# Ranking tokens for a top-64 selection: scores spread by TensorE, comparisons by key, counts as products with ones

## The reference

```python
def _L2_xattn_ref(query_seq, value_seq, router_w, q_w, kv_w, out_w):
    ...
    rw = jnp.einsum('bsd,od->bs', query_seq, router_w).astype(jnp.float32)
    top_w, top_idx = jax.lax.top_k(rw, C)
    resampled = jnp.take_along_axis(query_seq, top_idx[:, :, None], axis=1)
    q = jnp.einsum('bcd,ed->bce', resampled, q_w)
    ...
    q = q * _rope_factor(q_pos, d)
    ...
    att = jnp.einsum('bce,de->bcd', att, out_w)
    src = att * top_w[:, :, None]
    out = jnp.zeros_like(query_seq).at[jnp.arange(B)[:, None], top_idx].set(src)
    return out
```

## Time and profile before

| what | value |
|---|---|
| time, median of 3 runs | 2991.71 us |
| the three runs | 2980.21, 2994.35 and 2991.71 us |
| time of the profiled execution | 2995.15 us |
| span of the profiled execution | 2993.4 us |
| mean granted TensorE clock over the span | 0.893 of full speed |

### The profile page before, as it was taken

The page is one execution under the profiler, slowest core; times in us unless marked ns, Lnnn a source line. Parts: engine busy times, 40 slices in busy tenths (PEclk is TensorE's granted clock), DMA queues, the critical chain, the costliest instruction groups (busy, mean ns, idle before and its releaser), DMA issues. The chain is left out here.

```text
span 2993.4 us, 46160 instructions
## 1 busy us (share of the span) xinstructions
PE 2414.1 (81%) x16128; PEld 1491.5 (50%) x16128; DVE 1610.1 (54%) x3751; ACT 1283.7 (43%) x2885; POOL 922.6 (31%) x907
## 2 busy tenths in 40 slices
PE   2973676767667997899759889879999998399698
PEld 1432455345533444566437656546666665245465
DVE  5766764466455774333465444445555554566433
ACT  1652565346523665222224322246666665135222
POOL 2312772277203330000000000036777777054000
PEclk7986898789977998899879789989999999589799
DMA  5610000000004330000010000010000000042000
GB/s 140 79 18 6 1 1 1 0 1 1 1 8 103 44 43 1 15 0 0 0 48 1 1 30 0 0 62 1 1 1 1 1 1 1 11 46 33 1 0 14
DMA packets 49811, 53.80 MB, mean 18 GB/s; under 512 B 9264, under 2 KB 47920, under 8 KB 48720
## 3 DMA queue, kind: packets, MB, share of 16 engines
q1 hardware_dynamic: 42992, 41.68, 8.3%
q0 software_dynamic: 4896, 8.81, 1.0%
q10 hardware_dynamic: 1728, 0.79, 0.2%
HBM read 24.25 MB, written 1.05 MB: 8 GB/s over the span
## 5 line engine op out<-in xcount | busy, mean ns | idle before, releaser
L1958 POOL TENSOR_SCALAR L3x_prob<-L3x_prob,L3x_inverse 128x512 f32<-128x512 f32 x256 | 396.4, 1566 | 182.8 <-DVE L3x_inverse L2136 182.8
L1076 DVE TENSOR_TENSOR W_probT<-W_prob,W_pS 128x512 f32<-128x512 f32 (+1 forms) x232 | 159.4, 687 | 367.4 <-ACT W_prob L1059 367.4
L1059 ACT ACTIVATE W_prob<-W_pS 128x512 f32<-128x512 f32 (+1 forms) x232 | 138.6, 597 | 457.7 <-PE W_pS L1030 457.7
L1040 PEld LDWEIGHTS W_pT<-fw,W_probT 128*128 128x128 f32 (+1 forms) x1856 | 242.0, 191 | 116.0 <-issue 107.5
L1029 PE MATMUL W_pS<-hT,fw 128*128 (+1 forms) x464 | 242.8, 605 | 26.1 <-DVEq L497 26.1
L1040 PE MATMUL W_pT<-fw,W_probT 128*128 128x128 f32 (+1 forms) x1856 | 246.2, 276 | 6.2 <-DVE W_probT L1076 6.2
L2098 DVE CUSTOM_DVE_ANT_0 L3x_prob<-L3x_pS,L3x_mask_now 128x512 f32<-128x512 f32 x256 | 166.1, 686 | 149.0 <-PE L3x_pS L1966 149.0
L1030 PE MATMUL W_pS<-hT,fw 128*128 (+1 forms) x464 | 240.0, 599 | 0.0
L2043 ACT ACTIVATE L3x_prob<-L3x_prob,L3x_row_top 128x512 f32<-128x512 f32 x256 | 183.2, 717 | 72.3 <-DVE L3x_row_top L2098 72.3
L871 DVE TENSOR_REDUCE L1x_row_top<-L1x_pS 128x2 f32<-128x1024 f32 x128 | 156.6, 1223 | 73.5 <-PE L1x_pS L686 72.9
L815 ACT ACTIVATE L1x_prob_by_key<-L1x_pX 128x512 f32<-128x512 f32 x256 | 148.6, 597 | 100.9 <-PE L1x_pX L693 99.8
(11 more groups left out here) (370 smaller groups left out, 5183.0 us busy)
## 6 DMA issues: line engine op xcount, KB each, us to landing
L0x_key_stack<-xw SPq DMA_DIRECT2D x48, 128.0 KB
L1x_key_stack<-xw SPq DMA_DIRECT2D x96, 64.0 KB
L3f_stacks<-L3f_qk_part SPq DMA_DIRECT2D x96, 64.0 KB
fw<-in_f_L3f SPq DMA_DIRECT2D x1, 4483.5 KB, 13.5
fw<-in_f_L1f POOLq DMA_DIRECT2D x1, 4359.0 KB, 18.9
fw<-in_f_L0f POOLq DMA_DIRECT2D x1, 3890.0 KB, 15.4
fw<-in_f_L2f SPq DMA_DIRECT2D x1, 3460.0 KB, 10.8
L0x_query_stack<-xw SPq DMA_DIRECT2D x42, 64.0 KB
```

Source lines behind the costliest of these rows:

```text
L1040: last = pe.matmul(m.pT[:, e % 2, t * C:(t + 1) * C], hidden[0:size, s, t * P:(t + 1) * P], down(i), start=i == 0 and t == 0, stop=i == PI ...
L1059: act.activation(gated[0:size, s, 0:GROUP], prod[0:size, s, :], func, bias=bias).then_inc(activated, 1)
L1076: ins = dve.tensor_tensor(hidden[0:size, s, 0:GROUP], gated[0:size, s, 0:GROUP], prod[0:size, 2 + s, :], ALU.mult)
L1958: pool.tensor_scalar(prob(u, h, t), prob(u, h, t), m.inverse[:, u % 2, h, t:t + 1], None, ALU.mult).then_inc(a.normed, 1)
```

## The change

The router's row becomes a 128 x 128 table whose columns are all the same, so that one set of four products with `hT` gives every token's score in every partition at once. DVE still picks the own scores out with the identity. Comparisons now have the other direction: partition `p` holds a key, and its 0/1 row says which tokens it precedes. They are made of `across` (keys of one tile against tokens of the other), `within` (the same tile, strict) and `ties` (same tile, equal, and an earlier key, by a 128 x 128 table `sooner` in place of `earlier`). They are written as 2-byte numbers, and TensorE sums them over the keys by products with a column of ones, 48 products into 16 columns of the bank `pG`. A copy of these columns is the rank. `sel`, its transposes, the projection and the rotary product go by groups of four tiles.

```diff
     "L1x": [("wq", C), ("wk", C), ("wv", C), ("wo", C), ("bq", 1), ("bk", 1), ("bv_row", C), ("bo_row", C)],
-    "L2x": [("wq", C), ("wk", C), ("wv", C), ("wo", C), ("router_row", C), ("l2_ropeq", QT * C),
-            ("l2_ropek", SK), ("own_head", L2_HEADS // 2), ("slot", 2 * L2_CAP), ("earlier", QT * S)],
+    "L2x": [("wq", C), ("wk", C), ("wv", C), ("wo", C), ("router_wide", C), ("l2_ropeq", QT * C),
+            ("l2_ropek", SK), ("own_head", L2_HEADS // 2), ("slot", 2 * L2_CAP), ("sooner", P)],
...
+        every = m.banks.rearrange("p a n -> p (a n)").rearrange("p (b t j) -> p b t j", b=B, t=QT)
+        own = m.route[:, :].rearrange("p (b t) -> p b t", t=QT)
+        part = lambda n: m.kT[:, 2 * n:2 * n + 2, :].rearrange("p c n -> p (c n)").bitcast(BF16)[:, 0:TOK].rearrange(
+            "p (b t j) -> p b t j", b=B, t=QT)
+        across, within, ties = part(0), part(1), part(2)
+        same = m.v[:, 0, 0:TOK // 2].rearrange("p (b t j) -> p b t j", b=B // 2, t=QT)
...
         def _(pe):
-            pe.wait_ge(diagonal, 1)
             for g in range(4):
-                last = pe.matmul(m.banks[:, g, :], m.ones[:, :], wide(m.h)[:, g * 512:(g + 1) * 512], start=True,
-                                 stop=True)
+                last = pe.matmul(m.banks[:, g, :], w["router_wide"], m.hT[:, g * 512:(g + 1) * 512], start=True, stop=True)
             last.then_inc(spread, 1)
-            pe.wait_ge(picked, 1)
+            pe.wait_ge(compared, 1)
+            for b in range(B):
+                for t in range(QT):
+                    at = b * QT + t
+                    pe.matmul(m.pG[:, at:at + 1], across[:, b, t, :], m.onesb[:, 0:1], start=at == 0, stop=False,
+                              skip_group_check=True)
+                    pe.matmul(m.pG[:, at:at + 1], within[:, b, t, :], m.onesb[:, 0:1], start=False, stop=False,
+                              skip_group_check=True)
+            for half in range(2):
+                pe.wait_ge(tied, half + 1)
+                for b in range(4 * half, 4 * half + 4):
+                    for t in range(QT):
+                        at = b * QT + t
+                        last = pe.matmul(m.pG[:, at:at + 1], ties[:, b, t, :], m.onesb[:, 0:1], start=False, stop=True,
+                                         skip_group_check=True)
+            last.then_inc(ranked, 1)
             for g in range(4):
+                pe.wait_ge(picked, g + 1)
                 for t in range(4):
                     last = pe.transpose(m.banks[:, g, t * P:(t + 1) * P], sel[:, 4 * g + t, :], m.k["ident"])
                 last.then_inc(turned, 1)
...
-            last.then_inc(queries, 1)
+                last.then_inc(queries, 1)
...
-            st.done(dve.tensor_tensor(m.h[:, :, :], m.xn[:, :, :], row(w["router_row"], TILES), ALU.mult))
-            st.done(dve.tensor_reduce(m.route[:, :], m.h[:, :, :], AX_X, ALU.add))
-            dve.tensor_tensor(m.h[:, :, :], ident, each(m.route[:, :], P), ALU.mult).then_inc(diagonal, 1)
             dve.wait_ge(spread, 1)
-
-            st.done(dve.tensor_tensor(m.o[:, :, :], m.banks.rearrange("p a (t c) -> p (a t) c", c=P), ident,
-                                      ALU.mult))
-            st.done(dve.tensor_reduce(m.own[:, :], m.o[:, :, :], AX_X, ALU.add))
-            own = each(m.own[:, :].rearrange("p (b t) -> p b t", t=QT), S)
-            for b in range(2):
-                at = slice(4 * b, 4 * b + 4)
-                other = every[:, at, :].unsqueeze(2).broadcast_to([P, 4, QT, S])
-                mine = own[:, at]
-                for n in range(4):
-                    st.done(dve.tensor_tensor(more[:, 4 * b + n], other[:, n], mine[:, n], ALU.is_gt))
-                    st.done(dve.tensor_tensor(same[:, 4 * b + n], other[:, n], mine[:, n], ALU.is_equal))
-            earlier = w["earlier"].rearrange("p (t j) -> p t j", t=QT).unsqueeze(1).broadcast_to([P, B, QT, S])
-            st.done(dve.tensor_tensor(same, same, earlier, ALU.mult))
-            st.done(dve.tensor_tensor(more, more, same, ALU.add))
-            st.done(dve.tensor_reduce(m.own[:, :].rearrange("p (b t) -> p b t", t=QT), more, AX_X, ALU.add))
-            dve.tensor_tensor(sel, row(w["slot"], TILES), each(m.own[:, :], 2 * L2_CAP), ALU.is_equal).then_inc(picked, 1)
+            st.done(dve.tensor_tensor(m.o[:, :, :], m.banks.rearrange("p a (t c) -> p (a t) c", c=P), ident, ALU.mult))
+            st.done(dve.tensor_reduce(m.route[:, :], m.o[:, :, :], AX_X, ALU.add))
+            dve.tensor_tensor(across[:, :, 0, :], every[:, :, 0, :], each(own[:, :, 1], P), ALU.is_lt)
+            dve.tensor_tensor(across[:, :, 1, :], every[:, :, 1, :], each(own[:, :, 0], P), ALU.is_le)
+            dve.tensor_tensor(within, every, each(own, P), ALU.is_lt).then_inc(compared, 1)
+            sooner = w["sooner"].unsqueeze(1).unsqueeze(1).broadcast_to([P, B // 2, QT, P])
+            for half in range(2):
+                at = slice(4 * half, 4 * half + 4)
+                st.done(dve.tensor_tensor(same, every[:, at], each(own[:, at], P), ALU.is_equal))
+                last = dve.tensor_tensor(ties[:, at], same, sooner, ALU.mult)
+                last.then_inc(tied, 1)
+                dve.wait_ge(tied, half + 1)
+            dve.wait_ge(ranked, 1)
+            st.done(dve.tensor_copy(m.own[:, :], m.pG[:, 0:TILES]))
+            for g in range(4):
+                at = slice(4 * g, 4 * g + 4)
+                dve.tensor_tensor(sel[:, at, :], row(w["slot"], 4), each(m.own[:, at], 2 * L2_CAP),
+                                  ALU.is_equal).then_inc(picked, 1)
             turn_out_dve(dve, m, selT, turned, copied)
-            dve.wait_ge(queries, 1)
-            rope = w["l2_ropeq"].rearrange("p (n) -> p n").unsqueeze(1).broadcast_to([P, B, QT * C])
-            dve.tensor_tensor(wide(m.h).rearrange("p (b n) -> p b n", b=B),
-                              m.banks.rearrange("p a (b n) -> p (a b) n", b=2), rope, ALU.mult)
+            for g in range(4):
+                dve.wait_ge(queries, g + 1)
+                rope = w["l2_ropeq"].rearrange("p (n) -> p n").unsqueeze(1).broadcast_to([P, 2, QT * C])
+                dve.tensor_tensor(wide(m.h).rearrange("p (b n) -> p b n", b=B)[:, 2 * g:2 * g + 2, :],
+                                  m.banks[:, g, :].rearrange("p (b n) -> p b n", b=2), rope, ALU.mult).then_inc(roped, 1)
...
-                     tile2(k_at < q_at)]
+                     part[:, None] < part[None]]
...
-        "x_L2x": [L2x["q_w"].T, L2x["kv_w"][:C].T, L2x["kv_w"][C:].T, L2x["out_w"].T, rows(L2x["router_w"]),
+        "x_L2x": [L2x["q_w"].T, L2x["kv_w"][:C].T, L2x["kv_w"][C:].T, L2x["out_w"].T, rows(L2x["router_w"]).T,
```

More of the change, by code:

```diff
@@ L1632, in select_phase @@
     with Phase(nc, "L2x_select") as ph:
[L1633 to L1637, removed]
+        steps, spread, compared, tied, ranked, picked, turned, copied, queries, roped = (ph.sem(n) for n in (
+            "steps", "spread", "compared", "tied", "ranked", "picked", "turned", "copied", "queries", "roped"))
```

## The result

| | before | after |
|---|---|---|
| runs side by side on one chip | 4 | 4 |
| median | 2987.6 us (2980.21 to 2994.35) | 2952.45 us (2946.7 to 2962.18) |
| ratio, with its 95% interval | | 0.9892 (0.9863 to 0.992) |
| profiled execution | 2995.15 us | 2953.88 us |
| its span, mean granted clock | 2993.4 us, 0.893 | 2951.3 us, 0.906 |

The kernel is 35 us faster between the medians, and the interval of the ratio leaves out 1.

The account below looks back on a forecast made before the run. The selection was taken as one chain of DVE and TensorE in turn, 32.45 us in place of 55.16; with 1.0 behind it, 23.7 us less, 2971.4 profiled, 2968 as a median. Range 2956 to 2979 us.

Parts of the forecast that it names:

- the base: Whole kernel before: profiled 2995.15 us, 3.4 above the median of 2991.71, from which the gain was taken.
- Link 5: Selection, last eight ties: TensorE's products not hidden under DVE, with a semaphore, 1.1 us.
- Link 8: Selection, projection and rotary product: products 4.95 us, the mean of four examples, 5.7 with the last rotary quarter.
- Link 3: Selection, comparisons across and within: three DVE instructions from PSUM, 4.85 us.
- links 1, 2, 4, 6 and 7: Selection: spread 5.6 us, own scores 4.65, ties 5.05, copy of the ranks 0.3, slots and transposes 5.2.
- Link 9: Start of the attention behind the selection: shorter TensorE idle time, possibly a higher clock, gains 1.0 us.
- signs of being wrong: Wrong if comparisons exceed 1.3 ns a column, counts 0.126 us apart, or any later phase changes over a few us.
- Counts don't overlap: Selection: products adding into one column run one after another, costing 8.95 us more: 2977 us, chance 0.08.
- Clock stays low: Projection at the low clock's 6.97 us costs 2.0 more, next phase gains nothing: 2971 us, chance 0.12.
- Clock high throughout: Spread, last ties, transposes, products and next phase at the upper clock, 7 us less: 2961 us, chance 0.06.
- Gain swallowed: Selection: comparisons and ties, 9.9 us, cost 3.3 times that, bringing the time back to 2991 us; chance 0.05.
- Slower: Attention of the chosen tokens: clock held at 0.50, costing up to 120 us: 3088 us, chance 0.02.

Follow-up runs that it names:

- after, once more: The changed kernel, unedited, run again in more rounds against the kernel before: 2952.81 us, ratio 0.9901.
- counts only: The changed kernel with the old spread and without the groups of four, so only comparison by key and counts are new: 2975.09 us, ratio 0.9963.
- groups only: The kernel before with only slots, transposes, projection and rotary product by groups of four tiles: 2974.58 us, ratio 0.9956.
- more counts: The changed kernel with 320 more products with ones, into columns nobody reads: 2961.43 us, ratio 0.992.
- own scores by bank: The changed kernel with own scores picked out as each bank fills: 2951.43 us; with one DVE addition behind the last rotary quarter as well: 2950.27 us.
- old tables: The changed kernel with 384 columns of zeros behind its tables, giving them their old size: 2952.47 us, ratio 0.9902.
- null before: The kernel before, unedited, run again against itself: 2982.19 us, ratio 0.9994.
- later by one: The changed kernel with one unread DVE addition behind the last rotary quarter, starting the attention 0.6 us later: 2946.18 us, ratio 0.9879.
- kept busy: The changed kernel with nine unused 512-column products on TensorE while DVE compares: 2950.24 us, ratio 0.9869.

## Why the prediction fell short

The sign and the mechanism in the selection were right: one chain, shortened link by link. Three terms of the sum were wrong: the base was too high, the links were priced too dear, and what lies behind the phase was put too low, the fourth cross attention at nothing. 2968 against 2952.45 is 15.5 us. It comes apart so:

- **The base, 4 to 8 us.** The step was "It stands 3.4 above the median of 2991.71, so the forecast for a median is 2968". The median of three runs that spread over 14 us was taken as exact. Before stood at 2987.6 with one run more, and at 2983.78, 2986.76 and 2984.24 with 21, 9 and 11. The range made no room for this: it gave 5 us of scatter to its low end and none to the base. From the 2983.78 of 21 runs, 23.7 less would have read 2960.
- **The links, 2.6 us.** Link 5 was priced at 0.10 a product from 128-column products; one-column products come 0.027 apart. Link 8 was priced at the mean of four projections, and such a projection isn't a mean: it takes 3.84, or 5.5 to 6.2, by the clock. Link 3 was 0.38 too long: its three instructions are issued without a wait between them, and each starts 0.08 us before the record of the former ends (1480.60 and 1.22, then 1481.74), where 0.04 between instructions was charged. The rest, links 1, 2, 4, 6 and 7, is within 0.3 each.
- **Link 9, 2 us.** It was taken as 1.0 and is about 3.0: 1.6 in the attention, 2.0 in the router, and 0.3 and 0.2 lost in the phases between and behind. It named the right place (the start of the attention at the lower level) and missed two: the fall 34 us in, and the router.
- **`L3x`, 2.1 to 3.0 us.** Beyond link 9 the sum puts later phases at nothing, without a reason from rows. Its signs of being wrong name a later phase that changes by more than a few us; this one stays just inside that, and still is more than any link was off.
- **The rest, 0 to 5 us,** is within the size by which identical phases differ from one execution to the next (7.8 us between two profiles of before).

Sum of the parts: 25.3 in the selection, 3.0 in attention and router and 2.1 to 3.0 in `L3x` make 30.4 to 31.3, where 23.7 was forecast; the medians of before and after, once more, stand 31.0 apart. The 35.2 us of the first pair hold scatter besides.

**The rivals.** *Counts don't overlap* is refuted: 0.027 us a product is below a fourth of the 0.126 from which it would decide, though pairs add into one column. *Clock stays low* did not come in after, where the products behind the transposes ran at 1.00 as in the earlier trace rows; it did come in part in counts only, groups only, more counts and both kernels with own scores by bank, 5.47 to 5.82 us where the case had 6.97. The rows of before gave no way to tell which would come; after has 3.84 in all three profiles (also once more and with the old tables). By the Trainium skill's rule on transposes (TensorE: Matmul & The Clock Gate, Part 4: PE-mode transpose) it would come each time; the trace shows both, so the rule doesn't decide it. *Clock high throughout* came in part: the projection and the start of the attention yes (1.00), the spread (0.67) and most of the transposes no; the last ties were as short as that case had them, but at 0.50. *Gain swallowed* is refuted: links 3 and 4 took 9.46 us, not three times 9.9. *Slower* did not come: the clock does fall in the attention, but for 10 us and not for 120, and over the whole phase TensorE is at 0.50 for less time than before, as the next table shows.

**What the attention costs by the clock.** The time at 0.50 in each stretch is its length x 2 x (1 - granted clock):

```
                at 0.50 (us)                        attention   less half of it
null before     9.5 + 0.5 + 10.3 + 8.7 = 29.0       162.21      147.7
after           3.2 + 10.1 + 9.9       = 23.2       160.64      149.0
later by one    3.4 + 2.2              =  5.6       152.07      149.3
kept busy       3.4 + 10.4 + 22.8      = 36.6       166.76      148.5
```

The last column is flat within 1.6 us, so the attention is one amount of work, 148 to 149 us, and half of whatever time it spends at the lower level. The other ten profiles, reckoned from their clock records, lie between 147.7 and 149.4 as well. (The stretches not counted ran at 1.00; the 0.5 is from 1670.00 to 1673.40 at 0.92, the 3.4 of the last row from 1514.50 to 1520.00 at 0.69.) That accounts for the shift of 0.6 us, 8.8 by the table and 8.6 measured. Between before and after it gives 2.9 where 1.6 was measured; the other 1.3 is left over. What makes the clock fall at 1535.20 stays open. The stretch just ahead holds eight transposes and sixteen records of products of 16 columns at 1.00, but later by one, it holds them too and does not fall.

## What to carry to other kernels

Where two engines take turns in one chain, cost each link from its own row and trust the sum: eight links came within 2.6 us of 32. Take the base from as many runs as can be had, and put its uncertainty into the range, before refining links of a tenth of a microsecond. A phase dense in TensorE work is worth its work plus half of its time at the lower clock level, and a small shift of its start can change that by several microseconds (here 0.6 by 8.6), so time an edit also with its end moved by a microsecond. Look through the phases with unchanged code too: some 5 to 6 us of this change lie there.

## What the runs showed of the hardware

- One-column products of 2-byte numbers, each with a full weight load of its own, start 0.027 us apart at 0.50, though the record of each shows 165 ns and that of its load 104 ns: some six records lie over one another. The Trainium skill has a floor of about 25 ns from start to start (TensorE: Matmul & The Clock Gate, Part 1); the trace agrees with 27.
- DVE instructions without a wait between them overlap: 1.22, 1.21 and 2.28 us of records took 4.47, where the four that wait for each other took 4.99 for 4.89 of records. The Trainium skill (VectorE: DVE Perf Modes, The DRAIN you can't avoid) measured no gain from leaving the semaphores out between eight copies, and says in the same section that an instruction which is not held starts earlier. The trace shows the second: here it gained about 0.12 us for each instruction.
- The clock fell to 0.51 for 10.3 us with TensorE's records covering 10.30 of them, and in the 27.20 us ahead of it 27.12. A start 0.6 us later removed the fall.
